# Layer 1's bias goes into VectorE's copy of the values, the logits' shift becomes a 33rd column of the products, and all orders are laid out anew

## What is computed

```python
h = einsum('bnd,ade->bane', x, W);  th = tanh(h)
attn_src = einsum('bane,aeo->bano', th, w_src)
attn_dst = einsum('bane,aeo->bano', th, w_dst)
attn = attn_src + swapaxes(attn_dst, 2, 3)
attn = where(attn >= 0, attn, 0.2 * attn);  attn = where(~adj, -999.0, attn)
attn = softmax(attn, -1)
feat_out = einsum('banm,bame->bane', attn, h) + b
feat_out = elu(heads side by side)
gate = sigmoid(x @ H_w.T + H_b)
x = layernorm(x + gate * feat_out + (1 - gate) * x)
```

## Time and profile before

| what | value |
|---|---|
| median of 3 runs | 1103.05 us (1102.35 to 1104.42) |
| the profiled execution, its own time | 1102.98 us |
| its span, first to last instruction | 1101.1 us |
| busy in the span: PE, DVE, ACT, POOL | 1057.9, 872.4, 651.4, 704.2 us |
| last 89 us: PE busy | 67.7 us |
| mean granted clock of TensorE | 0.992 |
| one pass of the loop | 65.80 us |

### The profile page before, as it was taken

How to read it: one execution, slowest core, us unless ns; L and a number is a source line. 1 busy time by engine, 2 the same in 40 slices (tenths; PEclk the granted TensorE clock), 3 DMA queues, 4 the chain that set the end, 5 groups by cost and what they waited for, 6 DMA issues and landing times.

```text
span 1101.1 us, 28478 instructions
## 1 busy us (share of the span) xinstructions
PE 1057.9 (96%) x9226; PEld 894.6 (81%) x9226; DVE 872.4 (79%) x2289; ACT 651.4 (59%) x2060; POOL 704.2 (64%) x605
## 2 busy tenths in 40 slices
...
DMA packets 34722, 31.00 MB, mean 28 GB/s; under 512 B 15872, under 2 KB 34688, under 8 KB 34688
## 3 DMA queue, kind: packets, MB, share of 16 engines
...
...
## 4 chain that ended last, share of the span: by engine, by line
PE 79%; DVE 12%; issue 6%; ACT 1%; POOL 1%; DMA 0%; DVEq 0%; POOLq 0%; ACTq 0%
PE p_bank L577 50%; PE t_bank L716 4%; PE context L730 4%; DVE weights L1042 4%; PE scores L639 4%; PE context L736 4%; PE t_bank L648 3%; PE context L660 3%; PE t_bank L609 2%; PE t_bank L750 2%; PE t_bank L686 2%; DVE sd L1011 1%; DVE masked L950 1%; DVE neg_max L958 1%; PE t_bank L707 1%
## 5 line engine op out<-in xcount | busy, mean ns | idle before, releaser
L1149 POOL TENSOR_TENSOR w_rows<-qwT,own_head 96x1536 fp32r<-96x1536 f32 x64 | 179.8, 2809 | 87.8 <-ACT qwT L883 87.8
L1042 DVE SCALAR_TENSOR_TENSOR weights<-t_bank,pqw,clip 128x128 f32<-128x128 f32 x768 | 206.5, 343 | 7.4 <-PE t_bank L716 6.7
L1142 POOL TENSOR_TENSOR prod<-th,w_sd 128x768 f32<-128x768 f32 x64 | 118.3, 1848 | 124.9 <-ACT th L846 124.8
L818 ACT ACTIVATE probs<-masked,neg_max 128x128 f32<-128x128 f32 x384 | 148.8, 391 | 46.4 <-DVE neg_max L958 46.4
L577 PE MATMUL p_bank<-xT,w_q 128*128 128x512 f32 x432 | 113.7, 408 | 4.3 <-DVE w_k L927 4.3
L577 PE MATMUL p_bank<-w_v,xT 128*128 128x384 f32 x576 | 115.1, 344 | 1.2 <-DVE clip L995 1.2
L577 PE MATMUL p_bank<-w_f,cT 128*128 128x384 f32 x576 | 115.4, 344 | 0.4 <-DVE cT L920 0.4
L577 PE MATMUL p_bank<-w_h,x1T 128*128 128x384 f32 x576 | 113.8, 342 | 0.2 <-DVE x1T L920 0.2
L577 PE MATMUL p_bank<-w_g,x1T 128*128 128x384 f32 x576 | 113.1, 340 | 0.0
L577 PE MATMUL p_bank<-xT,w_k 128*128 128x512 f32 x432 | 111.4, 402 | 0.0
L1130 POOL TENSOR_TENSOR probs<-probs,rden 128x768 f32<-128x768 f32 x64 | 94.4, 1475 | 25.0 <-DVE rden L963 25.0
...
## 6 DMA issues: line engine op xcount, KB each, us to landing
...
```

The lines of the kernel that those rows point to most:

```text
L818: last = act.activation(probs0[:, k % 2, b, j * P:(j + 1) * P], masked[:, k % 2, b * PAIRS + j, :], ACT.Exp, bias=neg_max[:, b * PAIRS + j ...
L1042: last = dve.scalar_tensor_tensor(out=weights[:, g % 2, n, :], in0=src[:, i * P:(i + 1) * P], scalar=pqw[:, g % 2, 0, n:n + 1], in1=clip[: ...
L1142: pool.tensor_tensor(prod[:], over_heads(th[:], 2), w_sd[:], ALU.mult).then_inc(s_prod, 1)
L1149: pool.tensor_tensor(w_rows[0:QW_ROWS, k % 2], over_heads(qwT[:, k % 2, 1, :].bitcast(F32), H1), per_head(own_head[:], P), ALU.mult).then_ ...
```

## The change

Three things are done, apart from the orders:

1. `fb` is gone. Since the weights of a node are divided by their sum, a constant that is added to every value comes out added to the result; so the bias (less one, as before) is added to the values themselves. A new VectorE step `hb` reads `h` from PSUM, adds the bias and writes the SBUF copy that `pv1` reads. ScalarE's copy is gone, and `elu` and `mixa` read VectorE's `f_raw` result (`f_out`, two buffers).
2. `sda` is gone. `prod` becomes 24 rows of 33: the 33rd column holds the shift, written once at the start, and the sum over 33 columns gives the shifted logit.
3. All twelve tables have new orders.

```diff
-        prod = sb("prod", [P, 2, D])
-        sd = sb("sd", [P, 2, H1])
+        prod = sb("prod", [P, 2, H1, HD1 + 1])
-        f_raw = sb("f_raw", [P, D])
-        f_b = sb("f_b", [P, 2, D])
+        f_out = sb("f_out", [P, 2, D])
...
                     act.activation(th[:], src, ACT.Tanh).then_inc(s_th, 1)
-                    wait(act, pe["pv1"], upto(g1, GROUP, k - 1))
-                    act.activation(h[:, k % 2, :], src, ACT.Copy).then_inc(s_h, 1)
...
+                dve.tensor_scalar(prod[:, :, :, HD1], sd_shift[:], 1.0, None, ALU.mult).then_inc(s_shift, 1)
+                dve.wait_ge(s_shift, 4)
...
+                elif name == "hb":
+
+                    dve.wait_ge(s_th, upto(g1, GROUP, k + 1))
+                    if turn == SECOND and k == 0:
+                        dve.wait_ge(s_consts, 1)
+                    wait(dve, pe["pv1"], upto(g1, GROUP, k - 1))
+                    dve.tensor_tensor(h[:, k % 2, :].rearrange("p (h e) -> p h e", h=H1),
+                                      p_bank[p_at("h", k, turn)][:, 0:D].rearrange("p (h e) -> p h e", h=H1),
+                                      over_heads(bias_1[:], H1), ALU.add).then_inc(s_h, 1)
                 elif name == "sd":
 
                     dve.wait_ge(s_prod, upto(g1, GROUP, k + 1))
-                    wait(dve, s_sda, upto(g1, GROUP, k))
-                    dve.tensor_reduce(sd[:].rearrange("p a h -> p (a h)"),
-                                      prod[:].rearrange("p a (h e) -> p (a h) e", h=H1), AX_X,
-                                      ALU.add).then_inc(s_sd, 1)
-                elif name == "sda":
-                    dve.wait_ge(s_sd, upto(g1, GROUP, k + 1))
-
                     wait(dve, s_pqw, upto(g1, 3 * GROUP, 3 * k))
-                    dve.tensor_tensor(sda[:], sd[:], sd_shift[:], ALU.add).then_inc(s_sda, 1)
+                    dve.tensor_reduce(sda[:].rearrange("p a h -> p (a h)"),
+                                      prod[:].rearrange("p a h e -> p (a h) e"), AX_X, ALU.add).then_inc(s_sda, 1)
...
-                    pool.tensor_tensor(prod[:], over_heads(th[:], 2), w_sd[:], ALU.mult).then_inc(s_prod, 1)
+                    pool.tensor_tensor(prod[:, :, :, 0:HD1],
+                                       th[:].rearrange("p (h e) -> p h e", h=H1).unsqueeze(1).broadcast_to([P, 2, H1, HD1]),
+                                       w_sd[:].rearrange("p a (h e) -> p a h e", h=H1), ALU.mult).then_inc(s_prod, 1)
...
-                elif name == "fb":
-                    pool.wait_ge(s_fraw, upto(g1, GROUP, k + 1))
-                    wait(pool, s_mixb, upto(g1, GROUP, k - 1))
-                    pool.tensor_tensor(f_b[:, k % 2, :].rearrange("p (h e) -> p h e", h=H1),
-                                       f_raw[:].rearrange("p (h e) -> p h e", h=H1),
-                                       over_heads(bias_1[:], H1), ALU.add).then_inc(s_fb, 1)
```

Of the tables only a line stands here, from TensorE's loop:

```diff
-    ("qwT", 0), ("qk", 4), ("x1T", 2), ("qk", 5), ("gate", 1), ("s", 0), ("qwT", 1), ("wb", 0), ("v", 1), ("wb", 1),
+    ("qk", 4), ("qk", 5), ("qwT", 0), ("gate", 1), ("x1T", 2), ("s", 0), ("qwT", 1), ("v", 1), ("wb", 0), ("wb", 1),
```

More of the change, by code:

```diff
@@ L122 @@
+    ("gatet", 3, 1),
 ]
 DVE_LOOP = [
-    ("x1lo", 0), ("gsum", 0), ("x1lo", 1), ("sd", 0), ("sda", 0), ("wlog", 0), ("qwlo", 0), ("sd", 1), ("sda", 1),
-    ("wlog", 1), ("qwlo", 1), ("gsum", 1), ("x1lo", 2), ("mask", 0), ("e", 0), ("max", 0), ("e", 1), ("e", 2),
-    ("mask", 1), ("e", 3), ("e", 4), ("e", 5), ("rden0", 0), ("max", 1), ("rden1", 0), ("x1lo", 3), ("f_raw", 0),
-    ("sd", 2), ("sda", 2), ("rden0", 1), ("wlog", 2), ("gsum", 2), ("mask", 2), ("max", 2), ("sd", 3), ("sda", 3),
-    ("qwlo", 2), ("wlog", 3), ("mixa", 0), ("mixb", 0), ("qwlo", 3), ("sum1", 0), ("rden1", 1), ("clo", 0),
@@ L135 @@
[L135 to L137 removed]
+    ("x1lo", 0), ("hb", 0), ("x1lo", 1), ("gsum", 0), ("sd", 0), ("wlog", 0), ("hb", 1), ("qwlo", 0), ("sd", 1),
+    ("wlog", 1), ("qwlo", 1), ("gsum", 1), ("x1lo", 2), ("mask", 0), ("max", 0), ("e", 0), ("e", 1), ("e", 2),
+    ("mask", 1), ("rden0", 0), ("max", 1), ("sd", 2), ("x1lo", 3), ("e", 3), ("hb", 2), ("rden0", 1), ("e", 4),
@@ new lines @@
+    ("e", 5), ("wlog", 2), ("rden1", 0), ("f_raw", 0), ("mask", 2), ("gsum", 2), ("qwlo", 2), ("sd", 3), ("wlog", 3),
+    ("mixa", 0), ("max", 2), ("mask", 3), ("rden1", 1), ("clo", 0), ("f_raw", 1), ("hb", 3), ("mixb", 0), ("qwlo", 3),
+    ("rden0", 2), ("e", 6), ("max", 3), ("e", 7), ("sum0", 0), ("stats0", 0), ("e", 8), ("rden0", 3), ("mv0", 0),
+    ("sum1", 0), ("clo", 1), ("e", 9), ("stats1", 0), ("e", 10), ("e", 11), ("sum0", 1), ("mixa", 1), ("mv1", 0),
+    ("stats0", 1), ("clip", 0), ("rden1", 2), ("clo", 2), ("f_raw", 2), ("mixb", 1), ("out", 0), ("sum1", 1),
[4 rows of a table added]
@@ L138 @@
+    ("out", 3),
 ]
 DVE_BEGIN = [
[L141 to L145 removed]
```

198 lines of the change are left out of this document (95 added, 103 removed), and 106 rows, old and new, of tables (DVE_BEGIN, DVE_END, DVE_LOOP, PE_BEGIN).

## The result

The changed kernel took 1073.54 us (1072.93 to 1074.52, 4 runs), the kernel before 1103.72 beside it: a ratio of 0.9732, 95% interval 0.9721 to 0.9744. The gain is 30.2 us where 14.0 were forecast, and the time lies 0.5 us under the range. Its profiled execution took 1074.52, with a span of 1072.5 and a mean granted clock of 0.994. In the loop the clock was 1.00 throughout, before as after (183.88 to 973.54 us and 180.55 to 949.77), so none of the difference there is the clock's.

The account below looks back on a forecast made before the run. TensorE, 96% busy, was taken as the bound, losing time waiting for VectorE. Savings of 0.6 + 0.3 a pass over 13 passes (11.7), 0.9 in straight code and 1.35 at the end made 14.0: 1102.98 to 1089 us; range 1074 to 1107.

Parts of the forecast that it names:

- What bounds it: Whole kernel: TensorE, busy 96% of the span, is the bound; other engines count only where they make it wait.
- The loss of before: Old loop: TensorE loses 1.5 us a pass to VectorE's steps from `mask` 2 to `e` 8, 0.3 at the second `qwT`.
- the 0.9: New loop: TensorE still loses 0.9 us a pass to VectorE's steps from `mask` 1 to `e` 9, instead of 1.5.
- signs of being wrong: VectorE late when `s` 1 ends, steps waiting for `w_rows` or `prod`, `hb` delaying a projection, or ScalarE becoming the wait.
- The straight code: Code outside the loop, holding the rest of the layer 1 and layer 0 passes: one pass's saving, 0.9 us.
- The end: Last graph's chain: `elu` waits for `f_raw` alone, no longer for `f_b`; 1.35 us saved once.
- `sda` and the 0.3 at the second `qwT`: Loop: `sda` 1, held 1.45 us by GpSimd's `w_rows`, delays the second `qwT`; its removal saves 0.3 us a pass.
- rival on VectorE: VectorE stays the bound, its new 22 us stretch adding up small delays: 1098, or 1101 to 1103 us; chance 0.14.
- `wlog` 0's catch: Loop: GpSimd's `x_res` can hold `wlog` 0 for 2.5 us, but TensorE has other work meanwhile; costed at nothing.
- `hb`, `prod`, the sum, the 22 us of the run: Step times on VectorE and GpSimd: `hb` 0.55, `prod` 1.85, sum 0.97; VectorE's `mask` 1 to `e` 9 22.0 us.
- more than I count: Loop: separated `pT` and shrinking small TensorE losses save 2.1 us a pass, 28.7 with the end: 1074 us; chance 0.12.
- The catch in the run: GpSimd holds a VectorE step between `mask` 1 and `e` 9, costing 1.45 us a pass: 1109 us; chance 0.16.

Follow-up runs that it names:

- 4: Kernel before, with `pT` 5 in the loop moved behind `pv1` 2 and ScalarE's `pTo` 5 behind `elu` 1: 1112.45 us, ratio 1.0084.
- experiment 1: New arithmetic (`hb`, 33rd column, no `sda`, no `fb`, no ScalarE copy) in the orders of the kernel before: 1113.44 us, ratio 1.0093 to that kernel.
- 3: Changed kernel with the old orders in the straight code ahead of and behind the loop, new orders in the loop alone: 1086.99 us, ratio 0.9851.
- experiment 12: Kernel before, old arithmetic, with the new order of the loop's early stretch alone, up to the second `qwT`: 1116.01 us, ratio 1.0129.
- Experiment 7: Changed kernel with `sda` as a step of its own again behind the sum: 1087.01 us, ratio 0.9859 to the kernel before.
- Experiment 11: Changed kernel with TensorE's `qwT` 0 back ahead of `qk` 4 instead of behind `qk` 5: 1141.37 us, ratio 1.0350 to the kernel before.
- experiment 10: Changed kernel with `x_res` ahead of `prod` 0 on GpSimd, in the loop waiting until `out` 3 is made: 1070.86 us, ratio 0.9706.
- experiment 8: Changed kernel with `x_res` back behind the second `w_rows` in GpSimd's loop: 1098.97 us, ratio 0.9968 to the kernel before.
- experiment 15: Changed kernel with `mixa` 0 moved behind `max` 2, and `mixb` 0 and `sum1` 0 behind `e` 9: 1128.85 us, ratio 1.0244.

## Why the prediction was wrong

*What bounds it*: right. TensorE's waits are the whole matter; its busy share is 97%.

*The loss of before was undercounted; this step failed.* The prediction let TensorE lose 1.5 us a pass to VectorE's run and stopped at `e` 8. By the distances of the timeline it lost 0.85 more behind `e` 8, and 0.59 at the two `qwT` where 0.3 were counted (only the second was looked at, and against 0.22 instead of 0.14). That is 2.9 us instead of 1.8. What is left is also more than the 0.9: 0.42, 0.38 and some six waits of 0.1, about 1.4. 2.9 - 1.4 = 1.5 of the 1.71 us; the rest I have not assigned. Why the new order spares the 0.85 behind `e` 8 is read from the traces and not shown: the one experiment on it, 4, refuted my explanation. One of the prediction's own signs of being wrong also came: VectorE is already late when `s` 1 ends. That is at 471.0, and `mask` 1 starts at 471.50, behind `e` 2.

*The straight code*: 0.9 forecast. Measured were 3.33 + 3.56, less the thirteenth pass's 1.71 that lies in them: 5.2. "The saving of one pass" was too little for stretches of 1101.1 - 13 x 65.8 = 246 us. Experiments 1 and 3 show that its orders matter, 13.5 us between two ways to lay it out, but one of these has my `hb` in tables made without it. What the changed straight code saves step by step was not followed, and stays open. A part can be the clock's: from the last pass on the mean granted clock was 0.93 before (973.6 to 1101 us) and is 0.95 now (949.8 to 1072.4).

*The account*: 13 x 1.71 = 22.2 in the loop where 11.7 were forecast, 5.2 where 0.9, 1.27 where 1.35; together 28.7, the difference of the spans. The rest of the 30.2 lies between profiled executions and medians: the changed kernel's took 1.0 us more than its median, and that of the kernel before 0.7 less than the 1103.72.

*The end*: 1.35 forecast, 1.27 measured; right.

*`sda` and the 0.3 at the second `qwT`*: the catch was read rightly, but not what ends it. Without `sda` in the old orders (experiment 1) `wlog` 1 is caught instead and the second `qwT` still takes 0.52; with `sda` in the new early orders (experiment 12) it takes 0.18. So the 0.3 came from the later places, which the prediction let "add nothing that I can price", and it was right by luck to count it. In the new orders `sda`'s removal was priced too low. Experiment 7 gives 13.5 us for 64 `sda` in the new orders: 0.32 each in the run by the wait for the step ahead, and all of `pqw` 0 held. The prediction's rival on VectorE counted 0.12.

*`wlog` 0's catch, at nothing for a cover*: right, and the cover can be named. It is the later place of `qwT` 0 again. Experiment 11 prices it at 68 us, the clock's share included, and experiment 10 prices the covered catch at 2.7.

*`hb`, `prod`, the sum, the 22 us of the run*: right to 0.2 us.

*Adding the parts up*: this is the deeper fault, and no term of the sum. The prediction gave every part its own small saving. Alone, the arithmetic costs 10 us (half of it at the end, where I placed `hb`), the orders cost 68 (with `fb` and the copies where I placed them), the early stretch costs 13.5; together they gain 30. `fb` gone lets `elu` 0 stand early on ScalarE; `x_res` early keeps `prod` 2 in time (experiment 8, 25 us) and needs the late `qwT` 0.

*The rivals*: "more than I count" (0.12, 1074) came true, for one of its two reasons, the small losses. Its other reason, `pT` apart, was refuted as a gain by itself for `pT` 5 and not tried for the rest. That its 28.7 is what was measured is luck: it had 27.3 in the loop and nothing in the straight code, and 22.2 and 5.2 came. The catch in the run did not happen, though experiment 15 shows it one step away. Of `qwlo` the prediction said that none was caught so far; `qwlo` 0 now is (1.48), outside the run and covered.

The Trainium skill (GPSIMD Engine Reference, Specifications) names as contending the VectorE instructions with two SBUF inputs or in a two-port mode. The runs agree for `sda`, `qwlo` and `mixa`, which have two SBUF inputs and were held. `wlog` and `out` have one SBUF tensor and were held too; whether they ran in such a mode no run here shows. `hb`, which reads PSUM and one SBUF tensor, was not held: it took 0.55 at 485.20, inside `w_rows` (482.79 to 485.54).
